# Another order of events in three layers of a decoder kernel: gated attention, state space and wedge scores

## The chip, the cores and the metric

The program runs on one core of one Trainium2 chip. It is one launch that computes six layers one after the other for 8 sequences of 512 tokens with 256 features, all in 32-bit floats. The metric is the device time of the launch in microseconds (us); less is better. The engines of the core are called PE (TensorE: matmuls and transposes), DVE (VectorE), ACT (ScalarE), POOL (GpSimd) and SP (SyncE, which here only starts transfers).

## What is computed

After each layer the input of the layer is added to its result and a layer norm follows. The layers are, in order: gated linear attention with an MLP ("gla"), softmax attention over a context ("xattn"), a mixture of experts ("moe"), a state space layer ("mamba"), attention with wedge scores ("psi"), and a gated MLP ("ffn"). The change touches gla, mamba and psi. Cut to what matters:

```python
# gla: q, k, v, g = projections of xn = layernorm(x)
gk = log_sigmoid(xn @ Wgk1 @ Wgk2 + bgk2) / 16
h = h * exp(gt)[..., None] + kt[..., :, None] * vt[..., None, :]   # scan over tokens
o = einsum('bhk,bhkv->bhv', qt, h)
o = rmsnorm(o) * silu(g) @ Wo;  x = x + o
h = leaky_relu(layernorm(x) @ W1 + b1) ** 2;  x = x + h @ W2 + b2
# mamba: z, x_ssm, B, C, dt = rmsnorm(x) @ in_proj.T
x_conv = silu(conv of width 4 over tokens of x_ssm)
h = h * dA_t + dtx_t * B_t;  y_t = einsum('bhpn,bhn->bhp', h, C_t)  # scan
out = x + ((y + D * xh) * silu(z)) @ out_proj.T
# psi: features of Q and K from exp, sin and cos of a projection
wedge = sqrt(max(gram - tensor ** 2 - spinor ** 2, 0) + 1e-6)
w = softmax((g0 * wedge + g1 * tensor + g2 * spinor + g3 * hodge) / 4 / temperature)
out = (w @ V) @ Wo.T + bo
```

## The kernel before

A sequence (called a batch here, `b`) is worked on as a whole: its 512 tokens are 4 tiles of 128 partitions. Both scans are done in chunks of 128 tokens: in gla `scores` and `o` are the part within a chunk and the sum with the state, `dh` is the update of the state (`gla_Hs`), `kdT` a transpose that `dh` needs. In mamba `spread` and `masked` make the decays within a chunk (`mamba_intra`, and `inter`, which lies in the room `weights_even`), `add` updates the states, `y` multiplies, `gate` multiplies by silu(z), `conv` is the convolution, `out` the output projection, whose result DVE adds into `rows_kept`. In psi a `score` event is one tile of 128 queries by 512 keys of one head; there are 16 (`GQ`) of them in a batch, each copied by ACT (Relu, then Sqrt) and combined by DVE into `scores`; `exp` takes the exponentials of four of them, `turn` transposes probabilities, `pv` multiplies by the values, `sums` and `spread` carry the reciprocals of the row sums to where `scaled` uses them.

Each of these layers has a generator `order()`. It yields events (name, batch, part), and every engine walks through the same list and does its own share of each event; events that concern two batches are interleaved, in gla and mamba batch `b` and the next one `c`, in psi up to four. So the list fixes, by hand, the order of instructions on each engine; between engines there are semaphores only. An engine runs its instructions strictly in the order of the list, and a wait holds up all that stands behind it.

Results of PE go to four regions of PSUM. Three of them form the ring "short", in which the n-th result waits until the result three places earlier has been copied out (`claim`); in mamba the two halves of the fourth are the ring "bank", where the distance is two. So a change of the list also changes which copy a matmul waits for.

ACT has to load a table of functions before it changes between some functions. The loads (ACT_TABLE_LOAD) are put in by the build, at places that follow from ACT's order.

In gla the chain that this case turns on is: `z` (PE) to Abs on ACT, `soft` (Exp and Ln on ACT, giving a softplus), `sums` (a scan and differences on DVE), `exps` (ACT), `decayed` (DVE), then `kdT`, `dh`, `scores`, `o`. The MLP of the batch before runs beside it: `mlp` (PE, copied by ACT), `leaky` (DVE, then a Square on ACT), `out` (PE).

## Time and profile before

| | |
|---|---|
| median of 3 runs | 3025.9 us (3025.11 to 3036.9) |
| the profiled execution | 3040.14 us, of which the trace spans 3038.4 us |
| mean granted TensorE clock | 0.906 of full |
| instructions | 31582 |
| busy over the span | PE 2553.0 us (84%), DVE 1637.5 (54%), ACT 1384.5 (46%), POOL 321.4 (11%) |

The rows further down come from the profiled execution. It is one execution; its time is 14.2 us above the median. In a row of the trace in order of time stand the start in us, the duration, the engine, the line of the kernel, the operation and what it writes and reads; in brackets the idle time of the engine just before, and what ended it. A row with "x8" merges eight neighbouring instructions; a 32-bit matmul of 512 columns leaves two records. The windows give, for a stretch, its length, the busy time of PE, PEld (weight loads), DVE, ACT and POOL with the numbers of instructions, the granted clock, the share of the DMA engines, and GB/s. Gla runs from the start of the span to about 645 us, mamba's batches from about 1717 to 2127, psi from about 2147 to 2752. A granted clock of 1.00 is 2.4 GHz, 0.50 is 1.2 GHz.

### The profile page before, as it was taken

The numbers are of one execution on the slowest core, as the hardware profiler recorded it, in microseconds if no ns is written. First come the engines' busy times: TensorE is split into PE (matmuls) and PEld (weight loads), VectorE is DVE, ScalarE is ACT, GpSimd is POOL, SyncE is SP. The second block draws the span as 40 slices with busy tenths as digits, with TensorE's granted clock in tenths as the row PEclk, the third lists the DMA queues.
The fourth block names the chain that finished last, engine by engine and source line by source line (L and its number), as shares of the span: only waits on it lengthen the run. The fifth ranks groups of instructions, "written<-read, shape, count | busy, mean of one in ns | idle before, by whom it ended". The sixth has DMA issues, their size and how long they took to land. (4 is left out here: it accounts for less than half of the span.)

```text
span 3038.4 us, 31582 instructions
## 1 busy us (share of the span) xinstructions
PE 2553.0 (84%) x11456; PEld 1496.7 (49%) x11456; DVE 1637.5 (54%) x3416; ACT 1384.5 (46%) x1989; POOL 321.4 (11%) x299
## 2 busy tenths in 40 slices
PE   5888888865888888879999788886688888887998
PEld 3555566552333333355455455554344445444555
DVE  5555655644666666715443778877545555542222
ACT  2333333311555555532221856563377777872221
POOL 0001011000000000000166100000211111000000
PEclk8888988976999999979799899998799999988999
DMA  2000000005333333240035311211200010001000
GB/s 72 7 14 14 15 14 14 7 7 154 53 64 64 65 65 57 48 151 0 26 65 76 75 52 42 63 36 49 95 7 29 28 34 30 15 15 63 14 21 21
DMA packets 104947, 132.42 MB, mean 44 GB/s; under 512 B 21749, under 2 KB 87557, under 8 KB 104793
## 3 DMA queue, kind: packets, MB, share of 16 engines
q1 hardware_dynamic: 90440, 115.58, 14.3%
q0 software_dynamic: 11904, 14.69, 3.0%
q8 instruction: 92, 1.51, 0.2%
q14 instruction: 63, 0.51, 0.1%
q10 hardware_dynamic: 2448, 0.14, 0.1%
HBM read 73.69 MB, written 31.20 MB: 35 GB/s over the span
## 5 line engine op out<-in xcount | busy, mean ns | idle before, releaser
L986 DVE TENSOR_REDUCE xattn_tops<-region 128x2 f32<-128x1024 f32 x256 | 306.3, 1220 | 123.2 <-PE region L770 123.1
L923 ACT ACTIVATE xattn_probs<-region 128x1024 f32<-128x1024 f32 x256 | 256.2, 1022 | 125.0 <-PE region L759 124.0
L2126 PE MATMUL region<-psi_fT 128*128 128x512 f32 x512 | 250.0, 628 | 23.8 <-DVE psi_low L2402 14.4
L156 PE MATMUL region<-gla_xT,weights_even 128*128 128x512 f32 (+1 forms) x416 | 205.1, 646 | 29.7 <-ACT gla_xT L248 29.7
L759 PE MATMUL region<-xattn_qs,xattn_ks 49*128 49x512 f32 x512 | 125.8, 493 | 62.0 <-DVE xattn_tops L986 31.5
L156 PE MATMUL region<-mamba_xT,weights_odd 128*128 128x512 f32 x320 | 159.4, 646 | 3.9 <-DVE mamba_xh L1965 3.9
L2126 PEld LDWEIGHTS region<-psi_fT 128*128 128x128 f32 x512 | 94.5, 197 | 135.6 <-issue 102.5
L156 PEld LDWEIGHTS region<-gla_xT,weights_even 128*128 128x128 f32 (+1 forms) x416 | 77.6, 195 | 142.9 <-issue 108.6
L165 PE MATMUL region<-weights_even,gla_work 128*128 128x256 f32 x512 | 122.8, 401 | 25.9 <-ACT gla_work L519 24.5
L788 PE MATMUL region<-xattn_probs,xattn_va 128*32 128x512 f32 x1024 | 141.2, 619 | 1.1 <-ACT xattn_o_T L950 1.1
L770 PE MATMUL region<-xattn_ks,xattn_qs 48*128 48x512 f32 x512 | 124.4, 484 | 13.9 <-DMA xattn_ks<-xattn_khi 9.6
L2256 ACT ACTIVATE psi_wedge<-region 128x512 f32<-128x512 f32 x128 | 76.2, 595 | 120.1 <-PE region L2126 116.6
L1190 PE MATMUL region<-moe_xT,weights_even 128*128 128x512 f32 x256 | 126.7, 644 | 0.0
L165 PEld LDWEIGHTS region<-weights_even,gla_work 128*128 128x128 f32 x512 | 102.8, 202 | 48.2 <-ACT gla_work L519 28.2
L759 PEld LDWEIGHTS region<-xattn_qs,xattn_ks 49*128 49x128 f32 x512 | 48.6, 188 | 140.3 <-DVE xattn_tops L986 71.1
L770 PEld LDWEIGHTS region<-xattn_ks,xattn_qs 48*128 48x128 f32 x512 | 51.4, 197 | 131.3 <-issue 77.7
L2552 ACT ACTIVATE ffn_silu<-region 128x512 f32<-128x512 f32 x48 | 28.7, 597 | 187.5 <-PE region L2509 187.5
L506 ACT ACTIVATE gla_work<-region 128x1024 f32<-128x1024 f32 x8 | 8.2, 1024 | 228.7 <-PE region L413 228.7
L156 PEld LDWEIGHTS region<-mamba_xT,weights_odd 128*128 128x128 f32 x320 | 65.2, 209 | 87.1 <-issue 79.0
L2259 ACT ACTIVATE psi_wedge<-psi_wedge,psi_g_eps,psi_g_sq 128x512 f32<-128x512 f32 x128 | 104.1, 813 | 4.1
L2575 DVE TENSOR_TENSOR ffn_h<-ffn_silu,region 128x512 f32<-128x512 f32 x48 | 33.0, 687 | 131.3 <-ACT ffn_silu L2552 131.3
L2402 DVE CUSTOM_DVE_ANT_0 weights_even<-psi_wedge,region,psi_unsign 128x512 f32<-128x512 f32 x64 | 47.6, 747 | 92.7 <-ACT psi_wedge L2259 92.1
(501 smaller groups left out, 5225.6 us busy)
## 6 DMA issues: line engine op xcount, KB each, us to landing
weights_even<-mamba_cs SPq DMA_DIRECT2D x32, 512.0 KB, 4.8
xattn_qs<-xattn_qhi SPq DMA_DIRECT2D x128, 64.0 KB, 2.3
xattn_ks<-xattn_khi SPq DMA_DIRECT2D x128, 64.0 KB, 2.3
moe_sums<-moe_picked SPq DMA_DIRECT2D x9, 512.0 KB, 6.8
gla_x<-in_x SPq DMA_DIRECT2D x8, 512.0 KB, 3.8
x_after_gla<-gla_res SPq DMA_DIRECT2D x8, 512.0 KB, 2.9
xattn_x<-x_after_gla SPq DMA_DIRECT2D x8, 512.0 KB, 4.1
xattn_ctxT<-in_ctxT SPq DMA_DIRECT2D x8, 512.0 KB, 4.4
```

What stands on the lines that cost most here:

```text
L156: last = st.nc.tensor.matmul(o[0:m, i, :], w[:, c, col + i * P:col + i * P + m], rhs[:, c, :], start=c == 0, stop=c == kc - 1)
L165: last = st.nc.tensor.matmul(o[:, t * D:t * D + D], lhs[:, base + c, t * P:t * P + P], w[:, base + c, :], start=c == 0, stop=c == kc - 1)
L759: last = mm(o[:, r, :], ks[rows, ring(n), a, j * P:j * P + P], qs[rows, ring(n), a, :], start=True, stop=True)
L770: last = mm(o[:, r, :], qs[rows, ring(n), a, t * P:t * P + P], ks[rows, ring(n), a, :], start=True, stop=True)
L788: last = mm(o[32 * g:32 * g + 32, :], vas[b % 2][:, j, 2 * qd + r + 8 * a, :], probs[:, p % 3, a, r, :], start=j == 0, stop=j == NT - 1)
L923: A_(probs[:, p % 3, a, :, :], st.region(f"k{v}")[:], ACT.Exp).then_inc(st.emptying(f"k{v}"), 1)
L986: V.tensor_reduce(tops[:, n % 2, t, a::2], st.region(f"q{u}")[:], AX, ALU.max).then_inc(st.emptying(f"q{u}"), 1)
L1190: last = mm(o[:, a, :], w[:, c, (NE + i) * P:(NE + i) * P + P], xT[:, b, c, :], start=c == 0, stop=c == DC - 1)
L2126: last = mm(o[:, a, :], fT[:, h, 0, t * P:t * P + P], fT[:, h, 1 + a, :], start=True, stop=True)
L2256: A_(wedge[:, i % 2, :], st.region(f"s{b}_{i}")[:, 0, :], ACT.Relu).then_inc(st.sem("wedge_in"), 1)
L2259: A_(wedge[:, i % 2, :], wedge[:, i % 2, :], ACT.Sqrt, scale=g_sq[:], bias=g_eps[:]).then_inc(st.sem("wedge_root"), 1)
L2402: V.tensor_tensor_reduce(scores[b % 2][:, j, :], wedge[:, j % 2, :], st.region(f"s{b}_{j}")[:, 1, :], unsign[:], 1e30, ALU.add, ALU.min, l ...
```

## The change

Only the three lists change. Every event stays, and so does the work of each, with one exception that follows from ACT's order: the table loads, of which the whole program has 112 before and 89 after (33 and 25 in gla, 48 and 33 in mamba, as many as before elsewhere). In gla the key projection `k` moves on PE from between `onT` and `attn` to behind `xT2`; `soft` moves ahead of `g` on ACT; each `leaky` follows its `mlp`; the copy of `v` goes behind `exps`; `scores` 0 goes ahead of `dh`; and the `last` norm's moments go between the parts of `dh`. In mamba `out` moves behind the next batch's `xT`, `cb` and `dtxd`, and `masked` and `add` are spread out differently. In psi `pv` 0 goes ahead of `sums`, the four later `turn` events follow closely on each other, `sums` goes behind `score` 2, and the events in the exponential part are in another order.

```diff
--- before.py
+++ after.py
@@ -303,35 +303,36 @@
                 yield "low", c, 0
                 yield "q", c, 0
                 yield "onT", b, 0
-                yield "k", c, 0
                 yield "attn", b, 0
                 yield "second", b, 0
                 yield "z", c, 0
+                yield "soft", c, 0
                 yield "second", b, 1
                 yield "g", c, 0
                 yield "xT2", b, 0
-                yield "soft", c, 0
+                yield "k", c, 0
                 yield "mlp", b, 0
                 yield "sums", c, 0
+                yield "leaky", b, 0
                 yield "mlp", b, 1
+                yield "leaky", b, 1
                 yield "mlp", b, 2
-                yield "leaky", b, 0
-                yield "leaky", b, 1
-                yield "v", c, 0
                 yield "leaky", b, 2
                 yield "exps", c, 0
                 yield "decayed", c, 0
+                yield "v", c, 0
                 yield "out", b, 0
                 yield "kdT", c, 0
                 yield "last", b, 0
-                for i in range(NT - 1):
-                    yield "dh", c, i
                 yield "scores", c, 0
+                yield "dh", c, 0
+                yield "last", b, 1
+                yield "dh", c, 1
+                yield "dh", c, 2
+                yield "o", c, 0
                 yield "scores", c, 1
+                yield "scores", c, 2
                 yield "first", c + 1, 0
-                yield "o", c, 0
-                yield "scores", c, 2
-                yield "last", b, 1
                 yield "o", c, 1
                 yield "scores", c, 3
                 yield "first", c + 1, 1
@@ -1627,46 +1628,46 @@
             c = b + 1
             yield "spread", b, 0
             yield "dt", c, 0
+            yield "last", b - 1, 0
             yield "spread", b, 1
-            yield "last", b - 1, 0
+            yield "add", b, 0
             yield "soft", c, 0
             yield "spread", b, 2
-            yield "add", b, 0
-            yield "xs", c, 0
-            yield "spread", b, 3
             yield "last", b - 1, 1
             yield "add", b, 1
+            yield "xs", c, 0
+            yield "masked", b, 0
+            yield "spread", b, 3
             yield "steps", c, 0
+            yield "add", b, 2
             yield "xs", c, 1
-            yield "add", b, 2
-            yield "masked", b, 0
             yield "cs", c, 0
             yield "masked", b, 1
             yield "bcT", c, 0
             yield "y", b, 0
+            yield "csT", c, 0
             yield "conv", c, 0
             yield "masked", b, 2
-            yield "csT", c, 0
-            yield "fetch", c, 0
-            yield "conv", c, 1
             yield "masked", b, 3
             yield "moments", c + 1, 0
-            yield "cb", c, 0
+            yield "fetch", c, 0
+            yield "fetch", c, 1
+            yield "conv", c, 1
+            yield "z", c, 0
+            yield "gate", b, 0
+            yield "normed", c + 1, 0
+            yield "conv", c, 2
             yield "y", b, 1
-            yield "fetch", c, 1
-            yield "conv", c, 2
-            yield "gate", b, 0
-            yield "z", c, 0
             yield "conv", c, 3
-            yield "normed", c + 1, 0
             yield "z", c, 1
+            yield "b", c, 0
             yield "gate", b, 1
             yield "x_tok", c, 0
-            yield "b", c, 0
             yield "x_tok", c, 1
+            yield "xT", c + 1, 0
+            yield "cb", c, 0
+            yield "dtxd", c, 0
             yield "out", b, 0
-            yield "xT", c + 1, 0
-            yield "dtxd", c, 0
 
     work = [(what, b, i) for what, b, i in order() if 0 <= b < B]
 
@@ -2039,48 +2040,64 @@
 
         def order():
             for b in range(-2, B + 1):
-                for i in range(GQ):
-                    yield "score", b, i
-                    if i == 0:
-                        yield "sums", b - 1, 0
-                    if i == 1:
-                        yield "pv", b - 1, 0
-                    if i in (2, 4, 6, 7):
-                        yield "turn", b - 1, (2, 4, 6, 7).index(i) + 4
-                    if i == 3:
-                        yield "spread", b - 1, 0
-                    if i == 10:
-                        yield "pv", b - 1, 1
-                    if i in (9, 12):
-                        yield "scaled", b - 1, i // 12
-                    if i in (0, 1, 3, 5, 7, 9, 10):
-                        yield "features", b + 1, (0, 1, 3, 5, 7, 9, 10).index(i)
-                    if i == 3:
-                        yield "xT", b + 2, 0
-                    if i == 8:
-                        yield "Q", b + 2, 0
-                    if i == 11:
-                        yield "gen", b + 2, 0
-                    if i >= 12:
-                        yield "angles", b + 2, i - 12
-                yield "score", b, GQ
+                yield "score", b, 0
+                yield "features", b + 1, 0
+                yield "features", b + 1, 1
+                yield "pv", b - 1, 0
+                yield "score", b, 1
+                yield "score", b, 2
+                yield "sums", b - 1, 0
+                yield "score", b, 3
+                yield "features", b + 1, 2
+                yield "score", b, 4
+                yield "turn", b - 1, 4
+                yield "spread", b - 1, 0
+                yield "turn", b - 1, 5
+                yield "xT", b + 2, 0
+                yield "turn", b - 1, 6
+                yield "turn", b - 1, 7
+                yield "score", b, 5
+                yield "features", b + 1, 3
+                yield "score", b, 6
+                yield "score", b, 7
+                yield "score", b, 8
+                yield "features", b + 1, 4
+                yield "Q", b + 2, 0
+                yield "score", b, 9
+                yield "scaled", b - 1, 0
+                yield "features", b + 1, 5
+                yield "score", b, 10
+                yield "pv", b - 1, 1
+                yield "features", b + 1, 6
+                yield "score", b, 11
+                yield "gen", b + 2, 0
+                yield "score", b, 12
+                yield "scaled", b - 1, 1
+                yield "angles", b + 2, 0
+                yield "score", b, 13
+                yield "angles", b + 2, 1
+                yield "score", b, 14
+                yield "angles", b + 2, 2
+                yield "score", b, 15
+                yield "angles", b + 2, 3
+                yield "exp", b, 0
                 yield "growth", b + 2, 0
-                yield "exp", b, 0
                 yield "out", b - 1, 0
                 yield "fT", b + 1, 0
                 yield "exp", b, 1
+                yield "score", b, 16
                 yield "residual", b - 1, 0
+                yield "norm", b - 1, 0
                 yield "turn", b, 0
+                yield "exp", b, 2
                 yield "turn", b, 1
-                yield "norm", b - 1, 0
+                yield "turn", b, 2
                 yield "fT", b + 1, 1
-                yield "exp", b, 2
-                yield "turn", b, 2
-                yield "turn", b, 3
                 yield "fT", b + 1, 2
                 yield "exp", b, 3
+                yield "turn", b, 3
+                yield "sin", b + 2, 0
                 yield "fT", b + 1, 3
-                yield "sin", b + 2, 0
 
         work = [(what, b, i) for what, b, i in order() if 0 <= b < B]
```

The first place is ACT in gla, second batch: from the copy of `z` (L482 before, L483 after) to the Squares of `leaky` (L519, L520). Before:

```order
L482 ACTIVATE gla_work1<-region0,columns 128x512 x2
L486 ACT_TABLE_LOAD
L486 ACTIVATE gla_work1<-region1 128x1024
L248 ACTIVATE gla_xT0<-region2,columns 128x512 x2
L489 ACT_TABLE_LOAD
L489 ACTIVATE gla_work1<-gla_work1 128x1024
L491 ACT_TABLE_LOAD
L491 ACTIVATE gla_work1<-gla_work1 128x1024
L513 ACTIVATE gla_work0<-region0,columns 128x512
L514 ACTIVATE gla_work0<-region0,columns 128x512
```

After (the same lines have numbers one higher):

```order
L483 ACTIVATE gla_work1<-region2,columns 128x512 x2
L490 ACTIVATE gla_work1<-gla_work1 128x1024
L492 ACT_TABLE_LOAD
L492 ACTIVATE gla_work1<-gla_work1 128x1024
L487 ACT_TABLE_LOAD
L487 ACTIVATE gla_work1<-region0 128x1024
L248 ACTIVATE gla_xT0<-region1,columns 128x512 x2
L478 ACTIVATE gla_work1<-region2 128x1024
L514 ACTIVATE gla_work0<-region0,columns 128x512
L515 ACTIVATE gla_work0<-region0,columns 128x512
L520 ACTIVATE gla_work0<-gla_work0 128x1024
```

The Exp and Ln of `soft` now stand right behind the Abs of `z`, and the load ahead of Exp is gone; Silu (L486, now L487) and the copy of `xT2` (L248) come behind them, then the copy of `k`, and a Square of `leaky` follows each pair of MLP copies.

The second place is PE in mamba at the end of a batch: `mamba_xh` is what `x_tok` transposes (L1728, now L1729), L1700 (L1701) is the projection `b`, L165 is `out`, L148 is the next batch's `xT`, and L1687 (L1688) the next batch's `dt`. Before:

```order
L1728 MATMUL region1<-ident,mamba_xh1 128x128 x8
L1700 MATMUL region3<-weights_odd,mamba_xT 128x128 x8
L1728 MATMUL region2<-ident,mamba_xh1 128x128 x8
L165 MATMUL region0<-weights_odd,mamba_zs0 128x256 x16
L148 MATMUL region1<-ident,mamba_normed 128x128 x8
L1687 MATMUL region3<-weights_odd,mamba_xT 128x8 x8
```

After, with `cb` at L1720:

```order
L1701 MATMUL region3<-weights_odd,mamba_xT 128x128 x8
L1729 MATMUL region1<-ident,mamba_xh1 128x128 x8
L1729 MATMUL region2<-ident,mamba_xh1 128x128 x8
L148 MATMUL region0<-ident,mamba_normed 128x128 x8
L1720 MATMUL region3<-mamba_bct1 128x128 x4
L165 MATMUL region1<-weights_odd,mamba_zs0 128x256 x16
L1688 MATMUL region3<-weights_odd,mamba_xT 128x8 x8
```

`out`, which stood ahead of `xT`, is now behind it and behind `cb`, directly ahead of `dt`; `b` goes ahead of both transposes.

The third place is DVE in psi, where a batch's scores begin: L2414 is the copy of a `turn`, RECIPROCAL is DVE's share of `sums`, and an ISA row on `psi_wedge` is a score. Before:

```order
L2414 COPY psi_pT1<-region2 128x1024
L2414 COPY psi_pT1<-region0 128x1024
L2420 RECIPROCAL psi_recip<-psi_sums 128x16
L2322 TENSOR_TENSOR psi_tmp<-psi_gen,psi_growth 128x256
L2323 TENSOR_TENSOR psi_z<-psi_gen,psi_angle 128x32x8
L2324 TENSOR_TENSOR psi_z<-psi_gen,psi_angle 128x32x8
L2325 TENSOR_TENSOR psi_z<-psi_z,psi_tmp 128x32x8
L2402 ISA weights_even,psi_low<-psi_wedge,region0,psi_unsign 128x512
```

After (the score is L2419, the reciprocal L2437, and L2349 and L2351 are the end of `features` 1):

```order
L2349 TENSOR_REDUCE psi_n2<-psi_feat 128x32
L2351 TENSOR_TENSOR psi_feat<-psi_n2,psi_feat 128x16x8
L2419 ISA weights_even,psi_low<-psi_wedge,region0,psi_unsign 128x512
L2419 ISA psi_low 128x1
L2419 ISA weights_even,psi_low<-psi_wedge,region1,psi_unsign 128x512
L2419 ISA psi_low 128x1
L2437 RECIPROCAL psi_recip<-psi_sums 128x16
L2419 ISA weights_even,psi_low<-psi_wedge,region2,psi_unsign 128x512
L2419 ISA psi_low 128x1
```

The reciprocal stood ahead of everything of the new batch; now it is behind two parts of `features` and two scores.

## Rows read from the trace of the kernel before

**Rows 1.** Windows of six mamba batches and psi: length, busy PE, PEld, DVE, ACT, POOL.

```profile
1716.72:2031.25 314.53, 270.98 (x1574) 178.12 (x1573) 254.00 (x585) 186.62 (x248) 14.64 (x22) 0.95 0.15 50
2147.00:2752.00 605.00, 506.01 (x2269) 286.16 (x2267) 312.89 (x739) 419.59 (x718) 72.43 (x37) 0.94 0.07 24
```

**Rows 2.** Timeline of one batch of gla, from 241.34 to 316.56.

```profile
254.18 1.28 DVE L630 SCALAR_TENSOR_TENSOR gla_work<-region,rms_w,gla_work 128x1024 f32<-128x1024 f32 x1 [4.88 <-PE region L148]
...
257.42 3.62 PE L165 MATMUL region<-weights_even,gla_work 128*128 128x256 f32 x16
...
262.98 1.26 ACT L482 ACTIVATE gla_work<-region,columns 128x512 f32<-128x512 f32 x2 [4.34 <-PE region L368]
...
269.85 1.28 ACT L489 ACT_TABLE_LOAD   x1
269.89 10.57 PE L156 MATMUL region<-gla_xT,weights_even 128*128 128x512 f32 x24 [1.54 <-ACT gla_xT L248]
...
274.60 1.23 DVE L561 TENSOR_TENSOR gla_work<-gla_work 128x1024 f32<-128x1024 f32 x1 [6.27 <-ACT gla_work L491]
...
282.40 3.49 DVE L646 SCALAR_TENSOR_TENSOR gla_work<-gla_work 128x1024 f32<-128x1024 f32 x3
...
287.76 12.31 PE L165 MATMUL region<-weights_even,gla_work 128*128 128x256 f32 x48 [3.85 <-ACT gla_work L519]
...
293.65 1.23 DVE L580 TENSOR_TENSOR gla_work<-gla_work 128x1024 f32<-128x1024 f32 x1 [7.76 <-ACT gla_work L502]
...
302.99 0.68 PE L388 MATMUL region<-gla_work 128*128 128x128 f32 x4 [2.04 <-issue]
```

**Rows 3.** Windows from `kdT` to the next `xT`, five batches of gla.

```profile
216.00:241.34 25.34, 22.88 (x122) 20.88 (x121) 15.36 (x45) 0.00 (x0) 2.53 (x4) 0.58 0.03 9
299.91:316.56 16.65, 14.21 (x130) 12.85 (x128) 15.39 (x44) 0.00 (x0) 2.53 (x4) 1.00 0.00 1
372.17:398.61 26.44, 23.92 (x130) 21.79 (x128) 16.31 (x46) 0.00 (x0) 2.53 (x4) 0.59 0.03 10
452.65:480.87 28.22, 24.13 (x130) 22.00 (x129) 17.94 (x47) 0.00 (x0) 2.53 (x4) 0.61 0.03 9
534.91:554.73 19.82, 15.73 (x129) 14.15 (x129) 17.04 (x45) 0.00 (x0) 2.53 (x4) 0.91 0.00 1
```

**Rows 4.** Timeline of one batch of mamba.

```profile
1820.64 1.22 DVE L1973 SCALAR_TENSOR_TENSOR rows_kept<-rows_kept,region 128x1024 f32<-128x1024 f32 x1 [5.62 <-PE region L165]
...
1821.78 1.89 DVE L1922 TENSOR_TENSOR mamba_dtxd<-mamba_dtx,mamba_cs 128x512 f32<-128x512 f32 x3
...
1833.51 0.69 DVE L1940 TENSOR_TENSOR mamba_states<-mamba_states,mamba_cs 128x512 f32<-128x512 f32 x1 [0.52 <-PE region L1735]
...
1837.81 0.69 DVE L1940 TENSOR_TENSOR mamba_states<-mamba_states,mamba_cs 128x512 f32<-128x512 f32 x1 [2.55 <-PE region L1735]
...
1854.32 0.69 DVE L1904 TENSOR_TENSOR mamba_cbm<-region,tri 128x512 f32<-128x512 f32 x1
...
1863.41 1.23 DVE L1969 TENSOR_TENSOR mamba_zs<-mamba_zs,mamba_xh 128x1024 f32<-128x1024 f32 x1
...
1867.08 7.07 PE L165 MATMUL region<-weights_odd,mamba_zs 128*128 128x256 f32 x32
...
1876.44 1.95 PE L1687 MATMUL region<-weights_odd,mamba_xT 128*128 128x8 f32 x16 [1.41 <-ACT mamba_xT L248]
```

**Rows 5.** Timeline of psi: exponentials of one batch, then its successor's first scores.

```profile
2455.84 1.97 PE L2136 MATMUL region<-ident,weights_even 128*128 128x128 f32 x16 [1.68 <-ACT weights_even L2264]
...
2465.43 0.28 PE L2154 MATMUL region<-ident,psi_recip 128*16 128x128 f32 x1 [1.46 <-DVE psi_recip L2420]
...
2466.84 1.98 PE L2126 MATMUL region<-psi_fT 128*128 128x512 f32 x4 [1.13 <-ACT psi_fT L2250]
...
2472.14 0.81 ACT L2259 ACTIVATE psi_wedge<-psi_wedge,psi_g_eps,psi_g_sq 128x512 f32<-128x512 f32 x1
```

**Rows 6.** Windows of psi: two whole batches, from `out` to `out`.

```profile
2369.83:2445.08 75.25, 65.59 (x290) 36.35 (x289) 39.24 (x95) 52.58 (x90) 9.46 (x5) 0.93 0.10 29
2445.08:2516.14 71.06, 61.00 (x290) 34.89 (x289) 39.24 (x95) 52.57 (x90) 9.49 (x5) 1.00 0.09 30
```

## The prediction

> **What bounds the kernel now.** The profiled execution took 3040.1 us, 14.2 more than the median of the runs. The work is the same in both programs but for table loads, so only waits and PE's clock can change. I read the waits of each engine in the three layers first, then one batch of each in order of time, then the clock.
>
> In mamba DVE is the fullest engine beside PE: in six batches of together 314.53 us, 52.4 each, DVE is busy for 254.00 and PE for 270.98 [rows 1]. DVE is idle where it waits for `out` (5.62), and for PE's state updates (0.52 and 2.55) [rows 4]. What holds it there is PE's place in the list, not PE's work.
>
> In psi PE is busy for 506.01 of 605 us and ACT for 419.59 [rows 1]. They take turns: ACT sets the pace during the exponentials, PE during the scores.
>
> In gla the end of a batch hangs on a chain. The softplus is ready at 274.60, DVE's `sums` runs until the leaky part starts at 282.40, ACT's Squares follow, `out` starts on PE at 287.76 after a wait of 3.85, and only behind these Squares does ACT do `exps`, which release `decayed` at 293.65 [rows 2]. From there DVE is full until the next batch.
>
> **The clock in gla.** The stretch from `kdT` to the next batch's `xT` lasts 16.65 us at full clock and 19.82 at a mean of 0.91; in three of five batches it lasts 25.34, 26.44 and 28.22 at 0.58 to 0.61, with PE busy nearly all the time [rows 3]. The mean of the long ones, 26.7, is 8.4 above the mean of the other two. All have a PE wait near their start, such as the 2.04 us ahead of `dh` [rows 2]. The Trainium skill, "TensorE: Matmul & The Clock Gate", section on HAM oscillation, says that PE's clock is halved after idle time and comes back with sustained activity. The rows agree with the first half; the second they contradict for these light matmuls, since PE stays busy and slow for some 20 us. By the page's rule alone the clock term below would be nearly nothing and the time some 10 us higher.
>
> **Gla, step by step** (times of [rows 2]). (1) Without `k` ahead of it, `attn` waits for DVE's gated product: 254.18 + 1.28 = 255.5 instead of 257.4. It and `z` come 2.0 earlier, at the price of a new PE wait of about 1.3. (2) ACT's Abs of `z` ends at 264.24 now, so at 262.3; then Exp, one load (1.28) and Ln, about 1.1 for each activation (4.75 from 269.85 to 274.60 holds two loads and both). The softplus is ready at about 265.8, 8.8 earlier, and `sums` (274.60 to 282.40, 7.8) ends by about 274.6. (3) Silu with its load now stands ahead of the `xT2` copy; that copy ends near 269.7, as before. `k`, a third of the matmuls of `mlp` and so of their 10.57, 3.5 us on PE, covers the wait for it (1.54 now), so `mlp` starts at about 270.0 against 269.89 and ends 10.6 later, at 280.5. (4) The last `leaky` now waits for its own MLP copies and not for `sums`: 280.5, two copies of 0.7, a third of 3.49 on DVE, one Square of 1.05: 284.3. `out` starts there, 3.4 earlier, and `exps` too. `decayed` starts about 3.2 earlier (293.65 to 290.4). (5) After it DVE has the same work in another order until `xT`. `scores` 0 goes ahead of `dh` and starts as soon as `decayed` ends; later PE waits about 0.8 for a region that `dh` 1 has to empty, because the norm's moments are ahead of it on DVE. These cancel; bounds are 1 us better and 1 worse in each batch. So 3.2 per batch for seven batches with a successor: 22. The first batch has no MLP; there `z` comes ahead of `k` (3.6) and `soft` ahead of Silu and its load (2.3), of which I count 5. What would undo step 4 is queued behind `exps`: the copy of `v`, 1.0 us, for which `dh` waits; it ends at about 291.4, 8 us before `dh`.
>
> A rule on the loads: the row of one load has 1.28, and the next activation follows at once. "ScalarE: Activation LUTs" of the Trainium skill, section "What ACT_TABLE_LOAD costs", gives about 2.66 with the drain. By it the softplus would be ready at 267.2 and the sum the same, as `sums` would end at 275.9 and the last `leaky` still not wait for it.
>
> (6) Clock: PE now ends `out` before `kdT` can start (idle 1.2), then waits 1.4 for `decayed`; together more than the 2.04 now, though split. Against that, the `dh` matmuls, 128 columns by 128 rows, now come behind the light `scores` 0 and may bring the clock back, which light work alone did not. Three of five batches are 4.2 of seven now; I take three. Saved: 1.2 x 8.4 = 10. The ends are none of seven (35 saved) and all (24 lost). Gla: 22 + 5 + 10 = 37.
>
> **Mamba** (times of [rows 4]). (7) `cb` (0.69) and `dtxd` (1.89) move on DVE from the busy part into the wait for `out`. (8) `add` 1 and 2 stand on PE ahead of the long projections that DVE waited for; `masked` 0 and `spread` 3 stand ahead of `add` 2 on DVE. The waits of 0.52 and 2.55 go. Together 5.6 of the 44.0 from `rows_kept` (1820.64) to the end of the last `gate` (1863.41 + 1.23). (9) From there to the end of `out` at 1874.15 it is 9.5 now. In the new order the last `gate` is followed on PE by `xT` and `cb`, 1.0 each, ahead of `out`, but `b` (1.8) goes ahead: 9.5 again, with DVE waiting about 4. `dt` stands behind `out`, so its wait for the `xT` copy (1.41) is hidden. That gives 52.4 - 5.6 = 46.8 for an undisturbed batch. (10) PE's work is 270.98 / 6 = 45.2, so PE is nearly full. New waits are there: `cs` waits for `steps`, which stands behind `spread` 3 (about 2.1 after the second `xs`), `z` 1 for a region that `gate` 0 empties (0.2), `x_tok` for the last silu (0.8). I take 48.9, between 46.8 and 52.4 and nearer to what PE allows with these waits: 3.5 x 7 = 25. Bounds: 0 and 39. The queue of SP is moved little: the chunk sums are stored and fetched before DVE's next `spread`, with over 10 us to spare. The 15 loads fewer on ACT, at 1.28, save nothing: ACT is idle for 40% of mamba [rows 1].
>
> **Psi.** (11) `pv` 0, 3.6 us, now covers PE's waits of 1.46 (for the reciprocal) and 1.13 (for the last `fT`) [rows 5]. But the reciprocal now stands on DVE behind two scores. The second needs ACT's Sqrt, which ends at 2472.95; with 0.75 and 0.25 on DVE PE gets `sums` at 2474.0, having ended its second and third score, by the same walk from row to row, at 2471.8. A wait of 2.2 replaces 2.6, on the stretch in which PE sets the pace. (12) `turn` 2 goes ahead of `fT` 1 and waits for the exponentials: one wait of about 3 where PE had 1.68 and other short ones [rows 5]. ACT is the bound there, so this costs nothing by itself. But both long waits may halve the clock: a batch at clock 1.00 took 71.06 and one at 0.93 took 75.25 [rows 6]. Gain 0.4, clock risk about as large: 0 for eight batches, bounds 1.5 better and 4.2 worse each, of which I keep -12 to +20 in sum.
>
> **Sum.** 37 + 25 + 0 = 62 below 3040.1 is 2978. The profiled execution lies 14.2 above the median, by the same clock lottery or the profiler; I take a third of that off, so 2974, or 1.7% below the median of 3025.9.
>
> **Rivals.** (A) As forecast, all three terms of about this size: 2955 to 2994; chance 0.62. (B) PE becomes mamba's bound at once: its batches fall only to 51.4 and the clock in gla doesn't change: 3040 - 27 - 7 - 5 = 3001 (the 5 is the third of 14.2). For it speaks PE's 45.2 of 52.4, against it that PE's present waits are DVE's doing. 0.15. (C) The clock never stays halved in gla: 25 less than forecast, 2949; for it the 19.82 stretch, in which a halved clock did not stay, against it two PE waits at the very place. 0.08. (D) The clock is halved in every such stretch of gla: 4 x 8.4 = 34 more, 3008. 0.08. (E) Slower than before: psi's new waits ahead of `sums` and `turn` 2 halve the clock and it stays so through the scores, as it does in gla. At 8.4 a batch it costs 67: 3041. It decides if psi's batches grow by more than 6.5 each. Against it: scores are 512 columns wide, and 75.25 is the worst batch now. 0.07. That nothing changes is not a case of its own: the waits of steps 4 and 8 go in any order of the clock, and only a loss in psi near E's size could cancel them.
>
> The range 2946 to 3008 leaves out E, half of D and the lower part of C. About 0.5% (15 us) can be told from no change. Faster by more: A, B, C and most of D, 0.86; within: 0.08; slower: 0.06.
>
> **What would show it.** In gla: softplus ready some 10 us before the MLP's matmuls end; PE's wait ahead of `out` under 1 us; `exps` 3 us earlier; the stretch from `kdT` to `xT` as long as before at the same clock, and long in about three of seven. In mamba: 48 to 50 between one `xT` and the next, DVE's waits for the state updates gone and about 4 left ahead of `rows_kept`. In psi: a PE wait of about 2 ahead of `sums`, a batch within 71 to 75. I am wrong if PE's waits in mamba add to more than 6 a batch, or if gla's half-clock stretches are as many as before or more.

## The result, and the profile after

The changed kernel takes 2925.0 us in the median of four executions (2915.1 to 2935.8), the kernel before 3025.5 beside it: a ratio of 0.966, with the interval 0.963 to 0.968. I had forecast 2974, with 2946 to 3008 as the range. The sign was right, the gain was twice what I had worked out, and the time lies 21 us under the lower end.

In e7 (two), e10 (two) and e9 (one of twelve, 4571.6 us, which no trace here explains) single executions lie 60 us or more above the others of the same kernel, and the ratios leave them out.

The page of the profiled execution of the changed kernel (2915.1 us), its span and busy time:

```profile
span 2913.3 us, 31557 instructions
PE 2502.7 (86%) x11456; PEld 1482.0 (51%) x11456; DVE 1650.9 (57%) x3416; ACT 1352.2 (46%) x1966; POOL 327.7 (11%) x299
```

The two profiled executions differ by 125.1. The last batch of gla begins its `onT` at 585.6 and not 637.1 (51.4 earlier), mamba from its first `xT` to psi's first is 38.4 shorter (412.1 against 450.5), psi up to ffn 35.6 (598.0 against 633.6), and the rest agrees within 1. The traces exaggerate gla, since the one of before lies above its median and the one of after below.

One batch of gla after, in order of time, set against [rows 2]. The transposes `onT` began at 253.11 there and begin at 226.81 here, and times below count from them:

```profile
229.23 3.72 PE L165 MATMUL region<-weights_even,gla_work 128*128 128x256 f32 x16 [1.38 <-DVE gla_work L631]
...
238.56 1.06 ACT L492 ACTIVATE gla_work<-gla_work 128x1024 f32<-128x1024 f32 x1
...
240.17 1.22 DVE L562 TENSOR_TENSOR gla_work<-gla_work 128x1024 f32<-128x1024 f32 x1
...
245.02 3.02 DVE L574 TENSOR_TENSOR gla_work<-gla_work 128x256 f32<-128x256 f32 x4
...
257.85 10.63 PE L165 MATMUL region<-weights_even,gla_work 128*128 128x256 f32 x48 [0.39 <-ACT gla_work L520]
...
263.75 1.23 DVE L581 TENSOR_TENSOR gla_work<-gla_work 128x1024 f32<-128x1024 f32 x1 [7.04 <-ACT gla_work L503]
...
271.90 2.92 PE L399 MATMUL region<-weights_odd,gla_work 128*32 128x64 f32 x16 [2.51 <-DVE gla_work L594]
...
274.61 2.87 PE L389 MATMUL region<-gla_work 128*128 128x128 f32 x12
```

`attn` (the first row) comes after 2.4 and not 4.3, the softplus is ready after 12.8 and not 21.5, `sums` ends after 21.2 and not 29.3, `out` starts after 31.0 and not 34.7, `decayed` after 36.9 and not 40.5. The wait ahead of `out` fell from 3.85 to 0.39.

The windows from `kdT` to the next `xT`, as in [rows 3], now of the first batch and two more:

```profile
46.56:66.09 19.53, 17.90 (x129) 16.47 (x129) 13.92 (x33) 0.00 (x0) 1.27 (x2) 0.73 0.01 1
118.05:137.62 19.57, 17.06 (x130) 15.77 (x129) 17.05 (x44) 0.00 (x0) 2.53 (x4) 0.83 0.00 0
189.57:216.23 26.66, 24.15 (x129) 22.49 (x129) 18.13 (x47) 0.00 (x0) 2.53 (x4) 0.57 0.03 9
```

Of these seven stretches two are long (26.7 and 26.6 at 0.57 and 0.58), five last 19.1 to 19.6, four of them at a clock of 0.73 to 0.83. So in most short ones the clock is halved for a part of the stretch and comes back. In the trace of before four of seven were long, and the three short ones were at 0.78 (the first batch), 1.00 and 0.91.

Mamba after: one batch as a window, then rows of the next but one. `rows_kept` is L1974, the state updates L1941, `cb` L1905, `dtxd` L1923, `cs` L1707, and L156 is `z` 1:

```profile
1703.98:1750.99 47.01, 42.28 (x264) 28.41 (x263) 42.25 (x101) 28.56 (x40) 3.43 (x4) 1.00 0.17 57
```

```profile
1800.67 7.07 PE L165 MATMUL region<-weights_odd,mamba_zs 128*128 128x256 f32 x32
1800.87 0.69 DVE L1905 TENSOR_TENSOR mamba_cbm<-region,tri 128x512 f32<-128x512 f32 x1 [0.16 <-PE region L1720]
1801.47 1.89 DVE L1923 TENSOR_TENSOR mamba_dtxd<-mamba_dtx,mamba_cs 128x512 f32<-128x512 f32 x3
...
1807.78 1.22 DVE L1974 SCALAR_TENSOR_TENSOR rows_kept<-rows_kept,region 128x1024 f32<-128x1024 f32 x1 [4.42 <-PE region L165]
...
1816.55 0.69 DVE L1941 TENSOR_TENSOR mamba_states<-mamba_states,mamba_cs 128x512 f32<-128x512 f32 x1
...
1821.78 0.69 DVE L1941 TENSOR_TENSOR mamba_states<-mamba_states,mamba_cs 128x512 f32<-128x512 f32 x1
...
1821.91 0.41 PE L1707 MATMUL region<-mamba_dts,tri 128*128 128x32 f32 x2 [2.30 <-DVE mamba_dts L1883]
...
1837.74 3.70 PE L156 MATMUL region<-mamba_xT,weights_odd 128*128 128x512 f32 x8 [1.19 <-DVE mamba_xh L1966]
...
1844.77 1.22 DVE L1970 TENSOR_TENSOR mamba_zs<-mamba_zs,mamba_xh 128x1024 f32<-128x1024 f32 x1
```

From the third `xT` on, the distance between two is 47.0 to 47.1 in four batches and 47.9 in one (51.9 or 53.5 before). The one ahead of them, 39.4, holds no `out`, since `out` now stands behind `xT`. From `rows_kept` to the end of the last gate it is 38.2, and the waits ahead of the state updates are gone. In the window PE is busy for 42.28 at full clock, not for the 45.2 of [rows 1]; its waits are the other 4.7. The batch that took 47.9 ran at 0.93, with PE busy for 45.26.

Psi after, PE alone, one batch from its `out` at 2405.85 on. L2153 is `turn`, L2135 `fT`, L2143 a score (four records each), L2166 `pv`, L2171 `sums`, L2179 `spread`, L148 `xT`:

```profile
2411.80 1.97 PE L2153 MATMUL region<-ident,psi_scores 128*128 128x128 f32 x16 [1.45 <-ACT psi_scores L2281]
2416.62 1.09 PE L2153 MATMUL region<-ident,psi_scores 128*128 128x128 f32 x8 [2.86 <-ACT psi_scores L2281]
...
2421.14 1.10 PE L2135 MATMUL region<-ident,psi_feat 128*81 128x128 f32 x8 [0.81 <-ACT psi_fT L2267]
2422.93 1.95 PE L2143 MATMUL region<-psi_fT 128*128 128x512 f32 x4 [0.69 <-ACT psi_fT L2267]
2424.82 3.65 PE L2166 MATMUL region<-psi_pT,psi_ctxv 128*64 128x512 f32 x16
2428.40 3.70 PE L2143 MATMUL region<-psi_fT 128*128 128x512 f32 x8
2434.47 0.28 PE L2171 MATMUL region<-ident,psi_recip 128*16 128x128 f32 x1 [2.37 <-DVE psi_recip L2437]
2434.58 3.60 PE L2143 MATMUL region<-psi_fT 128*128 128x512 f32 x8
...
2444.43 7.03 PE L2143 MATMUL region<-psi_fT 128*128 128x512 f32 x16
2451.30 3.60 PE L156 MATMUL region<-psi_featT,weights_even 128*128 128x512 f32 x8
```

The reader is to see five named waits, 8.2 together, and none from 2434.58 to `Q` at 2451.30. The distance between two `out` is 68.8 once and then 68.2 three times in a row, where [rows 6] had 75.25 and 71.06.

### The profile page after: what moved, and what is told of

Read it like the earlier page. It is cut to its first block and busy times, and to the rows that moved or that the text cites. A ratio compares the mean times of both kernels' runs of the same rounds, so it can differ in the third digit from the quotient of the medians.

```text
span 2913.3 us, 31557 instructions
## 1 busy us (share of the span) xinstructions
PE 2502.7 (86%) x11456; PEld 1482.0 (51%) x11456; DVE 1650.9 (57%) x3416; ACT 1352.2 (46%) x1966; POOL 327.7 (11%) x299
## 5 line engine op out<-in xcount | busy, mean ns | idle before, releaser
L924 ACT ACTIVATE xattn_probs<-region 128x1024 f32<-128x1024 f32 x256 | 256.3, 1022 | 126.3 <-PE region L760 125.1
L2143 PE MATMUL region<-psi_fT 128*128 128x512 f32 x512 | 230.9, 597 | 10.3 <-ACT psi_fT L2267 7.1
L156 PE MATMUL region<-gla_xT,weights_even 128*128 128x512 f32 (+1 forms) x416 | 199.6, 634 | 20.2 <-ACT gla_xT L248 20.2
L2143 PEld LDWEIGHTS region<-psi_fT 128*128 128x128 f32 x512 | 93.6, 190 | 126.4 <-issue 115.0
L156 PE MATMUL region<-mamba_xT,weights_odd 128*128 128x512 f32 x320 | 154.2, 628 | 3.6 <-DVE mamba_xh L1966 3.6
L156 PEld LDWEIGHTS region<-gla_xT,weights_even 128*128 128x128 f32 (+1 forms) x416 | 77.1, 192 | 132.2 <-issue 106.1
L165 PE MATMUL region<-weights_even,gla_work 128*128 128x256 f32 x512 | 119.3, 393 | 17.6 <-DVE gla_work L631 11.0
L165 PEld LDWEIGHTS region<-weights_even,gla_work 128*128 128x128 f32 x512 | 99.2, 196 | 37.0 <-DVE gla_work L631 13.1
L2569 ACT ACTIVATE ffn_silu<-region 128x512 f32<-128x512 f32 x48 | 28.7, 597 | 187.0 <-PE region L2526 187.0
L156 PEld LDWEIGHTS region<-mamba_xT,weights_odd 128*128 128x128 f32 x320 | 62.4, 201 | 75.9 <-issue 71.4
L2526 PE MATMUL region<-ffn_xT,ffn_w_gate 128*128 128x512 f32 x192 | 91.9, 601 | 1.1 <-ACT ffn_xT L2563 1.1
```

What stands on the lines that cost most here:

```text
L156: last = st.nc.tensor.matmul(o[0:m, i, :], w[:, c, col + i * P:col + i * P + m], rhs[:, c, :], start=c == 0, stop=c == kc - 1)
L165: last = st.nc.tensor.matmul(o[:, t * D:t * D + D], lhs[:, base + c, t * P:t * P + P], w[:, base + c, :], start=c == 0, stop=c == kc - 1)
L924: A_(probs[:, p % 3, a, :, :], st.region(f"k{v}")[:], ACT.Exp).then_inc(st.emptying(f"k{v}"), 1)
L2143: last = mm(o[:, a, :], fT[:, h, 0, t * P:t * P + P], fT[:, h, 1 + a, :], start=True, stop=True)
L2526: last = mm(o[:, a, :], wide[n][:, c, e * P:e * P + P], xT[:, b % 2, c, :], start=c == 0, stop=c == DC - 1)
```

## The experiments

Every ratio is to the kernel before, executed in turn with the kernel on the same chip.

**e1, e2, e3: one layer's new order each.** The kernel before with the new order in gla, in mamba, or in psi alone.

> Only the gla list is the new one; mamba and psi keep the old. Theory S (the three layers' savings are separate and add up): 3025.5 minus 38 to 50, so 2975 to 2988; the stretch from kdT to the next xT is long (over 25 us) in two or three of seven batches. Theory F (the forecast's sum for gla was right and the rest came from elsewhere): minus 37 with the clock term, minus 27 without it, 2989 to 2998.

> Only the mamba list is the new one. Theory S: minus 36 to 40, 2986 to 2990, with 47 us from one xT of mamba to the next. Theory F (forecast): minus 25, 3000, with 48.9 us.

> Only the psi list is the new one. Theory S: minus 30 to 36, 2990 to 2996, batches of 68 to 70 us from out to out. Theory F (forecast): no change, 3025 plus or minus 10. A third way: psi gains only when the layers ahead leave the clock in another phase; then this run gains less than 15.

Measured: gla 0.987 (0.984 to 0.990), 40 us; mamba 0.987 (0.984 to 0.989), 40 us; psi 0.989 (0.986 to 0.991), 34 us. The sum, 114, agrees with the whole change (100 here, 112 in e11). So within the scatter the layers don't act on each other, gla is near the forecast (37), mamba gives 15 more than forecast, and psi 34 where I had nothing.

Psi in e1, with the old order, is the fair comparison for psi: a batch of 71.06 at clock 1.00, `out` at 2456.24. Here L2137 is `turn`, L2119 `fT`, L2127 a score, L2150 `pv`, L2155 `sums`:

```profile
2462.49 1.97 PE L2137 MATMUL region<-ident,psi_scores 128*128 128x128 f32 x16 [1.76 <-ACT psi_scores L2265]
...
2467.00 1.97 PE L2137 MATMUL region<-ident,psi_scores 128*128 128x128 f32 x16 [1.68 <-ACT psi_scores L2265]
...
2471.95 1.10 PE L2119 MATMUL region<-ident,psi_feat 128*81 128x128 f32 x8 [2.11 <-DVE psi_pT L2415]
2473.17 1.95 PE L2127 MATMUL region<-psi_fT 128*128 128x512 f32 x4
2476.59 0.28 PE L2155 MATMUL region<-ident,psi_recip 128*16 128x128 f32 x1 [1.47 <-DVE psi_recip L2421]
2478.00 1.98 PE L2127 MATMUL region<-psi_fT 128*128 128x512 f32 x4 [1.13 <-ACT psi_fT L2251]
...
2486.75 1.98 PE L2127 MATMUL region<-psi_fT 128*128 128x512 f32 x4 [0.31 <-DVE psi_low L2403]
...
2500.02 1.98 PE L2127 MATMUL region<-psi_fT 128*128 128x512 f32 x4 [1.47 <-DVE psi_low L2403]
...
```

Seven named waits, 9.9 together, against 8.2 in the kernel after. The last one, 1.47 at 2500.02, is PE waiting after a `turn` for DVE to empty a score's region. `Q` comes 48.2 behind `out` and in the kernel after 45.4: 2.7 less, of which 1.7 are named waits and the rest, which I did not trace to its rows, short gaps. The first score starts 16.9 behind `out` here and 17.1 in the kernel after, and from `Q` to the next `out` it is 22.9 and 22.8. So the gain of a batch lies between its first score and `Q`, where the named waits fall from 4.4 to 2.4.

**e4: sums directly behind the first score again, in the kernel after.**

```diff
                 yield "score", b, 0
+                yield "sums", b - 1, 0
                 yield "features", b + 1, 0
                 yield "features", b + 1, 1
                 yield "pv", b - 1, 0
                 yield "score", b, 1
                 yield "score", b, 2
-                yield "sums", b - 1, 0
```

> The changed kernel, but in psi the event sums stands directly behind score 0 and ahead of pv 0, so DVE's reciprocal no longer stands behind two scores. If the PE wait of 2.4 us ahead of the transpose of the reciprocals is on the path that sets psi's pace: 1 to 2 us less per batch, 8 to 16 in all, 2909 to 2917. If the wait is cover for something that PE waits for anyway (the regions that ACT and DVE have to empty), or sums now waits ahead of pv 0 for the exponentials: the same time within 5, or up to 8 more.

Measured: 0.969 (0.966 to 0.972), slower than the kernel after by some 9 to 18 us, more than either case allowed. Psi's batches, from `out` to `out`, are back at 71.5 to 72.4. With `sums` early, a wait of 1.2 stands ahead of it, and others of 1.0 and 1.3 ahead of the third score and of `spread`. So the place of `sums` is needed for nearly the whole of psi's gain in a batch.

**e5, e6: the two parts of psi's new order.** e5 has the new list up to the last score and the old one from the exponentials on; e6 the reverse.

> The kernel before, with the new order only for the part of psi in which the scores are made (pv 0 ahead of sums, sums behind the third score, the other places of turn, spread, features, Q and scaled); the part with the exponentials stays as it was. Theory now: psi's gain is PE's, from this part: pv 0 covers two waits of together 2.6 a batch, and what replaces them is nearly all covered too, so that the distance between two batches falls from 72 to about 69 and psi gives about 23 of its 33 us: ratio 0.992. Rival 1 (my prediction's steps): a wait of 2.2 replaces 2.6 on PE's path, 0.4 a batch: ratio 0.999. Rival 2: the gain needs both parts, since each only moves the wait to the other: under 8 us.

> The kernel before, with the new order only for the part of psi with the exponentials (turn 2 ahead of fT 1, exp 2 ahead of turn 1, sin ahead of the last fT); the scores stay as they were. Theory now: ACT sets the pace here, so this gives what is left of psi's gain, 5 to 10 us, mostly in the last batch, where it is followed by nothing else: ratio 0.997 to 0.998. Rival 1 (my prediction's step 12): nothing, 1.000 to 1.001, with a risk of a halved clock. Rival 2: the whole of the gain comes from here, ratio 0.989.

Measured: e5 0.996 (0.994 to 0.998), 12 us faster; e6 1.004 (1.002 to 1.006), 11 us slower; both together are 34 faster. Rival 2 of e5 had the mechanism, that the gain needs both parts, but with under 8 us; that e6 would be slower nobody had. PE's rows of e5 from the last `fT` of a batch's exponentials on and, behind them, of e6 from the `fT` behind its long wait on:

```profile
2457.98 1.10 PE L2134 MATMUL region<-ident,psi_feat 128*81 128x128 f32 x8 [2.11 <-DVE psi_pT L2430]
2459.20 3.55 PE L2142 MATMUL region<-psi_fT 128*128 128x512 f32 x4
2462.68 3.70 PE L2165 MATMUL region<-psi_pT,psi_ctxv 128*64 128x512 f32 x16
...
```

```profile
2375.14 2.70 PE L2118 MATMUL region<-ident,psi_feat 128*81 128x128 f32 x16
...
2383.67 0.28 PE L2154 MATMUL region<-ident,psi_recip 128*16 128x128 f32 x1 [1.20 <-DVE psi_recip L2420]
2387.01 3.65 PE L2126 MATMUL region<-psi_fT 128*128 128x512 f32 x4 [3.07 <-ACT psi_fT L2250]
```

In e5 the old exponentials still have their three waits of 1.7 to 2.1, and the first score takes 3.55, twice its 1.95: half clock. In e6 the last `fT` is copied late by ACT, as `sin` now stands ahead of it, and the second score waits 3.07 for that copy, where it was 1.13. With `pv` 0 ahead of it, as in the kernel after, that wait is covered. e6's batches last 74.9 to 75.1 at a clock of 0.95.

**e13: only the turns put together, in the kernel before.**

```diff
-                    if i in (2, 4, 6, 7):
-                        yield "turn", b - 1, (2, 4, 6, 7).index(i) + 4
-                    if i == 3:
-                        yield "spread", b - 1, 0
+                    if i == 4:
+                        yield "turn", b - 1, 4
+                        yield "spread", b - 1, 0
+                        yield "turn", b - 1, 5
+                        yield "xT", b + 2, 0
+                        yield "turn", b - 1, 6
+                        yield "turn", b - 1, 7
```

> The kernel before, with psi's turns 4 to 7, spread and xT put together behind the fifth score, as the new order has them (turn, spread, turn, xT, turn, turn), in place of one between every two scores; sums and pv 0 stay. Theory: the scattered turns cost PE two waits for a score region (1.47 behind s4 and 1.47 behind s6, as DVE has to empty it) and some 0.1 to 0.2 at each change between matmul and transpose; my prediction's steps 11 and 12 left this group of moves out. Then this gives 1.5 to 2.5 a batch, 12 to 20 us, ratio 0.994 to 0.996. Rival: what the new scores part gave alone (2.3 a batch) comes from pv 0 ahead of sums, and the waits behind the turns are made up for at the next score: under 4 us, ratio 0.999.

Measured: 0.999 (0.997 to 1.000): 3 us at most, not told from nothing. The rival holds. PE's waits of 0.31 and 1.47 do go, but here is what follows the grouping:

```profile
2394.09 1.96 PE L2163 MATMUL region<-psi_recipT,ident 16*64 16x128 f32 x32 [1.31 <-DVE psi_low L2403]
...
2398.60 2.76 PE L2137 MATMUL region<-ident,psi_scores 128*128 128x128 f32 x16
```

A wait of 1.31 ahead of `spread`, and two turns that take 2.76 where the kernel after has 1.91 for the same sixteen transposes: half clock again.

**e8: the reciprocal two scores earlier, in the kernel after.** DVE does it at the place of `pv` 0; PE's order stays.

```diff
-                    elif what == "sums":
+                    elif what == "pv" and i == 0:
                         dve.wait_ge(st.sem("exped"), GH * (b + 1))
```

> The kernel after, with psi's reciprocal done on DVE at the place of pv 0, two scores earlier in DVE's queue; the list and PE's order stay. It takes away the wait of 2.37 ahead of the matmul of sums. Theory: PE sets the pace from the first score to out, so each batch gets 2 us shorter (68.2 to about 66), in sum 14 to 18 us: ratio to the kernel before about 0.961. Rival: the wait was hidden, since ACT's Relu and Sqrt, one pair of 1.4 for each score, set the pace there and PE meets their regions a little later: then no change against the kernel after, ratio 0.966, and the wait only moves to the next score.

Measured: 0.963 (0.960 to 0.966), and e11, the kernel after again, 0.963. The rival holds, and psi's batches are still 68.2. PE's rows:

```profile
2286.87 3.70 PE L2143 MATMUL region<-psi_fT 128*128 128x512 f32 x8
2291.53 0.27 PE L2171 MATMUL region<-ident,psi_recip 128*16 128x128 f32 x1 [0.96 <-DVE psi_low L2419]
2292.77 3.70 PE L2143 MATMUL region<-psi_fT 128*128 128x512 f32 x8 [0.96 <-DVE psi_low L2419]
```

The wait of 2.37 became two of 0.96 for regions that DVE's scores empty. Here they hold PE nearly as long as the reciprocal did: the fourth and fifth scores start 28.4 behind `out`, and started 28.7 behind it in the kernel after.

**e7, e15, e10: the two parts of gla's new order.** e7 is the kernel before with the new order up to `last` 0 (k, soft, leaky, v), e15 the kernel before with the new order behind it (scores 0 ahead of dh, last 1 early), e10 the kernel after with the old order behind it:

```diff
                 yield "last", b, 0
+                for i in range(NT - 1):
+                    yield "dh", c, i
                 yield "scores", c, 0
-                yield "dh", c, 0
-                yield "last", b, 1
-                yield "dh", c, 1
-                yield "dh", c, 2
...
```

> The kernel before, with the new order of gla only up to the first last (k behind attn and g, soft ahead of second 1, leaky between the mlp parts, v behind decayed); scores, dh and o keep the old order. Theory (the prediction's steps 1 to 4): this alone starts decayed 3.2 earlier in each batch and gives 5 in the first, 27 in all, and the new back part gives only the clock, so this run's gain is 25 to 30 us, ratio 0.991, with the stretch from kdT to xT long in as many batches as before (about half). Rival 1: the back part is worth something at full clock too, since the periods at full clock fell by 3.7 and not by 3.2: then this run gives only 20. Rival 2: the back part costs something (with it the way from exps to xT is 1.2 us longer): then this run gains as much as or more than the full order of gla, 40 us, ratio 0.987.

> The kernel before, with the new order of gla only in its back part (scores 0 ahead of dh 0, last 1 and the other scores as in the kernel after). Theory (the prediction's steps 5 and 6): nothing at full clock, and one or two stretches fewer at half clock: 5 to 12 us faster, ratio 0.996 to 0.998. Rival 1: it costs 1.2 a batch in the way from exps to the next xT, as the kernel after showed against the kernel before: 5 to 8 us slower, 1.002. Rival 2: with the old front part, where decayed starts late, the wait ahead of scores 0 comes after the wait for out and more stretches than before run at half clock: over 10 us slower.

> The kernel after, with the old order of gla's back part (dh 0 to 2 ahead of scores 0, last 1 behind scores 2); all else as in the kernel after. Theory: at full clock the two back parts differ by 0.3 a batch (71.8 against 71.5), so this tells the clock term of the prediction (step 6) by itself. If the new back part brings the clock back sooner, as I counted with 10 us, this run is 5 to 15 slower than the kernel after. Rival: the two runs with one of each back part gave 44 and 40 us, so the old one loses nothing: the same time or up to 5 us faster than the kernel after in the same batch of runs.

Measured: e7 0.983 (0.980 to 0.986), 52 us, even more than its rival 2 had; e15 0.996 (0.994 to 0.999), 12 us; e10 0.962 (0.960 to 0.963) beside e11's 0.963 (0.961 to 0.965). By these ratios the front part is the whole gain, and behind it the new back part gives nothing; only ahead of the old front is it worth 12 us, and there none of the seven stretches of the trace is over 21.3. But the ratios leave out two of six executions of e7 (3054.8 and 3054.9, the others 2974 to 2993) and two of seven of e10 (2979.6 and 2983.3, the others 2906 to 2919). The profiled execution of e10 is one of these; e7's two are not traced. One of its batches from `onT` to `onT`, the stretch from `kdT` to `xT` in it, and its `dh`:

```profile
168.36:250.24 81.88, 74.08 (x289) 51.58 (x288) 45.80 (x86) 27.75 (x34) 7.80 (x8) 0.79 0.04 13
...
209.85:238.44 28.59, 24.90 (x129) 22.78 (x129) 18.01 (x47) 0.00 (x0) 2.53 (x4) 0.57 0.02 8
```

```profile
214.61 3.16 PE L388 MATMUL region<-gla_work 128*128 128x128 f32 x12 [3.69 <-issue]
```

PE waits 3.69 ahead of `dh`, and the stretch from `kdT` to `xT` is long in all seven batches with a successor, and the six distances that follow the first batch are 81.8 to 81.9, where the short ones of e7 have 71.8. In the kernel after the same place has one shorter wait, 2.51 ahead of `scores` 0, and none ahead of `dh`. In the 27 executions of the kernel after (twice), e1, e4 and e8, which have the new back part behind the new front, no such time occurs, against four of 13 with the old back part. So the new back part seems to take away a chance of losing some 70 us: my case D, in the order that was not chosen. With all executions counted, e7's mean is 3007 and e1's 2993, e10's 2933 and e11's 2916. That the one long wait is what keeps the clock down is not shown: the executions of e10 without the loss have no trace.

**e12: soft behind xT2 again, in the kernel after.**

```diff
-                yield "soft", c, 0
                 yield "second", b, 1
                 yield "g", c, 0
                 yield "xT2", b, 0
+                yield "soft", c, 0
```

> The kernel after, with one edit undone in gla: soft stands behind xT2 again, not behind z. Theory (the prediction's steps 2 and 4): sums on DVE then end some 5 to 9 later and hold the last leaky and with it out, so each batch is 2 to 3.6 longer and the first batch some 2 to 3: 15 to 28 us more than the kernel after, ratio 0.971 to 0.976. Rival: the place of leaky between the mlp parts frees the last leaky from sums already, since ACT's Squares no longer queue behind; then this costs under 5 us, ratio 0.966 to 0.968, and the steps gave the gain to the wrong edit.

Measured: 0.977 (0.975 to 0.979), 42 us more than e11: the theory holds and was too small. Rows from `onT` at 237.78 on, DVE's `sums`, the last `leaky` and `out`:

```profile
257.49 1.23 DVE L562 TENSOR_TENSOR gla_work<-gla_work 128x1024 f32<-128x1024 f32 x1 [6.27 <-ACT gla_work L492]
...
272.29 1.22 DVE L647 SCALAR_TENSOR_TENSOR gla_work<-gla_work 128x1024 f32<-128x1024 f32 x1 [2.28 <-ACT gla_work L515]
...
```

```profile
274.66 12.73 PE L165 MATMUL region<-weights_even,gla_work 128*128 128x256 f32 x48 [6.23 <-ACT gla_work L520]
```

`out` waits 6.23 and starts 36.9 behind `onT`, not 31.0. On DVE all three `leaky` stand behind `sums`, in both kernels. Here `sums` ends 6.4 later, so the first `leaky` starts 5.8 later, and as each Square stands on ACT ahead of the next MLP copies, the delay reaches `out` whole. The 5.8 are 41 in seven batches.

**e9, e14: the two parts of mamba's new order.** e9 is the kernel before with only this:

```diff
-            yield "out", b, 0
             yield "xT", c + 1, 0
+            yield "cb", c, 0
             yield "dtxd", c, 0
+            yield "out", b, 0
```

(and `cb` away from its old place); e14 has the whole new order, but `out` ahead of `xT`.

> The kernel before, with one edit in mamba: out stands behind the next xT, cb and dtxd and not ahead of xT. Theory (the prediction's step 7): DVE does cb and dtxd, 2.6, in its wait for out, so the distance between two batches falls from 51.9 and 53.5 by 2.5 to 3; the whole of mamba gives 18 to 20 us of the 39 that its full order gives: ratio 0.994. Rival 1: the whole gain hangs on this edit, since the waits for the state updates were hidden: ratio 0.987. Rival 2: out now comes later on PE and holds up rows_kept on DVE, and only with the other edits ahead of it does this pay: no gain, 1.000, or a loss.

> The kernel before, with the whole new order of mamba but for out, which stands ahead of the next xT, cb and dtxd. Theory (the prediction's step 8 by itself): the waits of 0.52 and 2.55 for the state updates go and the gate parts stand closer: the full order gives 39, out's place alone 16 to 19, so this gives 15 to 23, ratio 0.993 to 0.995. Rival: the two parts need each other, as in psi: with out ahead, DVE waits for it with cb and dtxd behind it, and this gives under 8 us.

Measured: e9 0.995 (0.994 to 0.997), 14 us, batches of 49.5; e14 0.992 (0.989 to 0.994), 26 us, batches of 48.5. Together 40, the same as e2. Here the parts add up. Each theory had the mechanism; e9 gave less than its 18 to 20, though its batches are as short as forecast, and e14 somewhat more than its 15 to 23.

**e11: the kernel after again**, beside e9, e10 and e12.

> The kernel after, unchanged, beside the others of this set: it gives the scatter of its ratio from one set of runs to another, 0.963 to 0.969 by the theory that the scatter comes from how many of gla's stretches run at half clock. A ratio outside that would mean that differences of 3 us between kernels of different sets, which I have leaned on, mean nothing.

Measured: 0.963 (0.961 to 0.965), 2917.4 us. The first measurement gave 0.966 (0.963 to 0.968). A difference of 0.003 between sets says nothing. The two profiled executions, 2915.1 and 2906.1, fit the theory that gla's stretches make the scatter: the second has one long stretch of seven and not two, and is 6.1 of the 9.0 ahead at the end of gla.

## Why the prediction was right in sign and wrong in size

The forecast gains were 37, 25 and 0; alone the layers gave 40, 40 and 34.

**Gla, steps 1 to 4: right.** `attn` 1.9 earlier (2.0 forecast) behind a new wait of 1.38 (1.3); softplus 8.7 earlier (8.8); `sums` ends 8.1 earlier (forecast 7.8, though the step's own 265.8 + 7.8 is 273.6 and not 274.6); `mlp` unchanged, since `k` covers its wait; `out` 3.6 earlier (3.4) and `decayed` 3.6 (3.2). The first batch is 7.7 shorter, not 5: its `kdT` starts at 46.56 and not at 54.27. e12 shows that the early `soft` carries this chain. **Step 5: right.** Behind the new front, short batches last 71.8 with the old back part (e7) and 71.5 with the new one. At full clock the stretch from `kdT` to `xT` is 16.65 with the old back part ([rows 3]) and 16.66 with the new one (e12). **Step 6: right in direction and size, not in what decides.** The first window of [rows 3] starts 0.9 behind its `kdT`, and four of seven stretches were long in that execution. Over the traces of all runs, eight with gla's old order have 20 stretches of over 25 us (two to four of seven), five with the new order 7 (one or two): 1.1 fewer a run, forecast 1.2, though at a lower level than my 4.2 and three. The short batches fell from 75.2 to 71.5; by them 7.7 + 7 x 3.7 = 34 of e1's 40 come without the long ones, which leaves some 6 for the clock, forecast 10. That is an estimate, since the short batches are not all at one clock. The larger effect, that the old back part behind the new front sometimes keeps all seven long, I had only as case D.

**Mamba, steps 7 to 9: right.** 46.8 was the forecast for an undisturbed batch, 47.0 is measured; 38.4 and 38.2 from `rows_kept` to the last gate. **Step 10 failed.** I wrote "PE's work is 270.98 / 6 = 45.2, so PE is nearly full", and added 2.1 a batch for it. That busy time was taken at a clock of 0.95; at full clock the work is 42.28, and even a batch with 45.26 of it took only 47.9. The new waits came (2.30 ahead of `cs` where 2.1 was forecast, 0.91 and 0.8 ahead of `x_tok`, 1.19 and 0.2 ahead of `z` 1), 4.7 with all others, and 47.0 has room for them. This term was mis-sized by 15 us.

**Psi, steps 11 and 12, failed by what they left out**, 34 us of the error. (11) said "A wait of 2.2 replaces 2.6, on the stretch in which PE sets the pace". The exchange is there: 2.37 came for 1.47 and 1.13, worth 0.2 a batch, and e8 shows that removing the 2.37 would gain nothing more, as the regions then hold PE for two times 0.96. The step put the moves of `turn` 4 to 7 at nothing without a reason. In the whole new order the waits of 0.31 and 1.47 behind a `turn` and some 0.9 of short gaps are gone; by the rows they are most of a batch's gain. They go neither without the late `sums` (e4) nor by grouping the `turn` events alone (e13). I also left out the ends: from the trace of e1 to that of e3, 9.0 of psi's 34.2 lie ahead of the first `out` and 6.1 in the last batch, where the distance from `out` to the last `out` fell from 35.95 to 29.85. (12) said that the long wait ahead of `turn` 2 costs nothing by itself: right, 2.86 as forecast, and against my fear it halves nothing in the kernel after, where the batches run at 1.00. That they do depends on the rest of the list: the same wait in e6 is followed by half clock. For a batch at full clock the gain is 71.06 - 68.25 = 2.8; every second batch of e1 is at 0.98 and lasts 72.3, so the four whole batches give 13.4, and the two behind them 5.0. How the 2.8 splits among the moves stays open, since the parts alone give -12, +11 and -3 us (e5, e6, e13) and do not add.

**The rivals.** A's mechanism held for gla. B is refuted: mamba's batches fell to 47.0 and not to 51.4, and PE has 4.7 a batch to spare. C named the time that came nearest (2949) for the wrong reason: two stretches of seven are still long. D does occur, but with the old back part. E is refuted for the whole change. It is what e6 shows in small: new waits and the half clock behind them cost psi about 3 a batch there, not 8.4. Of the signs that I named, two failed: mamba's 48 to 50 (47.0) and psi's 71 to 75 (68.2).

On the rules cited: ACT's load still has 1.28 in its row and the next activation follows at once, 8.7 earlier as worked out by the row; by the 2.66 of the Trainium skill, "ScalarE: Activation LUTs", section "What ACT_TABLE_LOAD costs", it would be 7.4 by the prediction's estimate (267.2 against 274.60). On the clock, the rule of the Trainium skill that sustained activity brings it back ("TensorE: Matmul & The Clock Gate", section "What's actually happening") agrees with the stretches at 0.83, where it came back in the middle, and not with e10's, where PE is busy for 24.90 of 28.59 and stays slow.

## What to carry to other kernels

Busy time read at a lowered clock overstates an engine's need: take it from a stretch at full clock, and add the waits that would stay, before calling the engine full. A wait in a row costs time only if what stands behind it would not wait anyway; move the producer earlier, as e8 does, before pricing it. Where engines take turns, test the parts of a reordering together as well as alone: two halves that gave 12 us and cost 11 gave 34 together.

## What I had not expected of the hardware

The clock makes whole stretches of a layer fall into a pattern: in e10 six batches in a row last 81.8 to 81.9, each with the same long stretch at 0.57, and other executions of the same program take 60 to 75 us less. In e6 a wait of 2.86 and one of 1.45 before it were followed by half clock in the next 16 transposes (2.70), while the same two waits in the kernel after were not (1.91), though the rows around them are the same. Which of the two comes may hang on where the waits fall in time, but no run here varied that alone.
